# A graph network on one core: 38 more gathers behind the first pass's last one, and 32 small copies by SyncE with addresses from registers

## The reference

```python
def _gat_conv(x, src, dst, edge_attr, ...):          # twice, in the first network
    xs = (x @ lin_w.T).reshape(N, H, C)
    alpha = a_src[src] + a_dst[dst] + a_edge          # leaky ReLU follows
    m = jax.ops.segment_max(alpha, dst, num_segments=N)
    alpha = jnp.exp(alpha - m[dst])
    denom = jax.ops.segment_sum(alpha, dst, num_segments=N)
    msg = xs[src] * (alpha / (denom[dst] + 1e-16))[..., None]
    out = jax.ops.segment_sum(msg, dst, num_segments=N)
...
em = jnp.concatenate([x[src], x[dst]], axis=-1)       # once, in the second network
em = jax.nn.relu(layer_norm(em @ msg_w + msg_b, msg_g, msg_beta)) * edge_weights[:, None]
msgs = jax.ops.segment_sum(em, dst, num_segments=num_nodes)
```

## Time and profile before

| | |
|---|---|
| median of 3 runs | 8210.34 us |
| lowest and highest run | 8195.68 and 8234.33 us |
| span of the profiled execution | 6732.1 us |
| the profiled execution's own time | only its span is given |
| median less span | 1478.2 us |
| first pass, first to last of its gathers | 94.3 to 2141.3 us |
| instructions | 124645 |

### The profile page before, as it was taken

The page is one execution under the profiler, slowest core; times in us unless marked ns, Lnnn a source line. Parts: engine busy times, 40 slices in busy tenths (PEclk is TensorE's granted clock), DMA queues, the critical chain, the costliest instruction groups (busy, mean ns, idle before and its releaser), DMA issues. The chain is left out here.

```text
span 6732.1 us, 124645 instructions
## 1 busy us (share of the span) xinstructions
PE 5109.7 (76%) x33726; PEld 4567.4 (68%) x33726; DVE 4555.6 (68%) x15714; ACT 2981.2 (44%) x10333; POOL 4624.6 (69%) x4875
## 2 busy tenths in 40 slices
PE   5788887888887378888888888866676677776775
PEld 4666676676766268777777777856666666666664
DVE  5777777777777746666666665676666666666667
ACT  3444444444444322222222222255666666666666
POOL 4777777777775077777777777706777777777771
PEclk7788888888888656666666676679999999999997
DMA  8544444444443322222222222222222222222221
GB/s 173 151 116 115 115 112 114 115 115 115 114 114 85 103 61 63 64 62 63 63 63 62 64 62 63 62 86 60 54 54 53 54 54 54 54 54 54 54 54 29
DMA packets 334708, 534.90 MB, mean 79 GB/s; under 512 B 105502, under 2 KB 222767, under 8 KB 333665
## 3 DMA queue, kind: packets, MB, share of 16 engines
q0 software_dynamic: 181264, 439.20, 25.7%
q1 hardware_dynamic: 143462, 83.65, 4.6%
q10 hardware_dynamic: 9323, 4.08, 0.3%
HBM read 489.59 MB, written 42.61 MB: 79 GB/s over the span
## 5 line engine op out<-in xcount | busy, mean ns | idle before, releaser
L932 POOL DMA_INDIRECT arena<-rows,slot_src x3222 | 3079.0, 956 | 1027.3 <-issue 930.8
L722 POOL DMA_INDIRECT arena<-msg_rows,slot_src x1611 | 1521.4, 944 | 523.7 <-issue 483.9
L1130 ACT ACTIVATE arena<-psum 128x512 f32<-128x512 bf16 x808 | 480.2, 594 | 1552.3 <-PE psum L978 1528.4
L2034 PE MATMUL psum<-arena 128*128 x3232 | 704.9, 302 | 500.4 <-DMA arena<-msg_rows,slot_src 447.3
L1019 PE MATMUL psum<-arena 128*128 128x145 f32 x3232 | 978.6, 394 | 0.0
L1268 DVE TENSOR_TENSOR arena<-arena,psum 128x290 f32 x1616 | 731.2, 452 | 292.8 <-DVE arena L1268 176.6
L2034 PEld LDWEIGHTS psum<-arena 128*128 128x128 f32 x3232 | 524.6, 204 | 567.6 <-issue 567.4
L1021 PE MATMUL psum<-arena 128*128 128x145 f32 x3232 | 870.1, 360 | 0.0
L2041 ACT ACTIVATE arena<-psum 128x128 bf16<-128x128 f32 x1616 | 424.1, 277 | 754.5 <-PE psum L2036 754.4
L1205 DVE TENSOR_TENSOR arena<-arena,psum 128x512 f32<-128x512 f32 x808 | 553.6, 685 | 262.5 <-PE psum L1021 255.9
L1034 PE MATMUL psum<-arena 128*128 x3232 | 595.9, 326 | 155.9 <-ACT arena L1130 67.3
(11 more groups left out here) (360 smaller groups left out, 9590.5 us busy)
## 6 DMA issues: line engine op xcount, KB each, us to landing
arena<-rows,slot_src POOLq DMA_INDIRECT x3222
arena<-msg_rows,slot_src POOLq DMA_INDIRECT x1611
arena<-slot_keys SPq DMA_DIRECT2D x100, 128.0 KB
edge_alpha<-arena SPq DMA_DIRECT2D x50, 128.0 KB
arena<-edge_alpha SPq DMA_DIRECT2D x50, 128.0 KB
slot_keys<-lane_keys SPq DMA_DIRECT2D x24, 256.0 KB
arena<-rows SPq DMA_DIRECT2D x6, 1024.0 KB, 10.0
rows<-arena SPq DMA_DIRECT2D x4, 822.0 KB
```

The lines of the kernel that those rows point to most:

```text
L722: pool.indirect_dma_start(out=self.buffer[:, v % U, j, :], out_offset=None, in_=self.source, in_offset=bass.IndirectOffsetOnAxis(ap=K.SRC[ ...
L932: pool.indirect_dma_start(out=E.rowbuf[:, r, j, :], out_offset=None, in_=E.source, in_offset=bass.IndirectOffsetOnAxis(ap=K.SRC[:, at:at + ...
L1130: act.activation(E.onehotT[:, v % 2, :, :], E.psT, ACT.Copy).then_inc(E.turned, 1)
L2034: pe.matmul(psH[b][:, j, :], onehotT[:, b, j, :], K.by_dst[:, bass.ds(blocks(v, j), 1), :].rearrange("p b w -> p (b w)"), start=True, stop ...
```

## The change

Two functions are added, and two places call them. `spare_copies` runs in SP's queue at window 40 of the first pass, behind the wait on `topped` and ahead of the window's loads: four times it reads eight block numbers into SP's registers and issues eight copies of a_node's block of that number (128 partitions x 16 values) into `lane_keys`; then it waits for all 32. `spare_gathers` runs in POOL's queue behind the first pass's gathers: it waits for the copies, gathers 22 times from h0 into `lane_keys` (twice each: 128 rows of 128 values, and 128, 127, 126, 124, 120, 112, 96, 64, 32 and 16 rows of 64 values), waits for them, gathers 8 times 128 rows with a wait after each, then 8 times with two waits on reached semaphores and a step of a semaphore of its own ahead of each, and waits for the last. Nothing reads `lane_keys` afterwards. The semaphore is K.arrived[21]; two new ones are spare_copies and spare_steps. The SBUF table keeps its place and size.

```diff
+        self.spare = Relay(self.arrived[21], 16)
...
-        self.dstf = K.sb("lane_keys", [P, SC, P])[:, :, :]
+        lanes = K.sb("lane_keys", [P, SC, P])
+        self.dstf, K.dstf_lanes = lanes[:, :, :], lanes[:, :, :].rearrange("p c e -> p (c e)")
...
+            if E.first and z == 40:
+                spare_copies(E)
...
+def spare_copies(E):
+    sp, K = E.K.sp, E.K
+    E.keys_rest.after(sp)
+    copied = K.dmas("spare_copies")
+    lanes = K.dstf_lanes[:, 0:32 * 2 * H].rearrange("p (k w) -> p k w", k=32)
+    for n in range(4):
+        blocks = numbers_loaded(K, ET.SP, K.slot_blocks, n * LOADED, NB - 1)
+        for k in range(LOADED):
+            copied.done(sp.dma_start(lanes[:, n * LOADED + k, :].rearrange("p (b w) -> p b w", b=1),
+                                     K.a_node[:, bass.ds(blocks[k], 1), :]))
+    copied.after(sp)
+    K.spare_copied = copied
+
+def spare_gathers(E):
+    pool, K = E.K.pool, E.K
+    spare = K.spare
+    lanes = K.dstf_lanes
+    K.spare_copied.after(pool)
+    wide, half = K.h0, K.h0.rearrange("n (k w) -> (n k) w", k=2)
+    at = 0
+    for rows_, source, w in ((P, wide, F), (P, half, F // 2), (127, half, F // 2), (126, half, F // 2), (124, half, F // 2),
+                             (120, half, F // 2), (112, half, F // 2), (96, half, F // 2), (64, half, F // 2), (32, half, F // 2),
+                             (16, half, F // 2)):
+        for _ in range(2):
+            spare.done(pool.indirect_dma_start(out=lanes[0:rows_, at:at + w], out_offset=None, in_=source,
+                                               in_offset=bass.IndirectOffsetOnAxis(ap=K.SRC[0:rows_, 0:1], axis=0)))
+            at += w
+    spare.after(pool)
+    again, stepped = lanes[:, 0:F], K.sem("spare_steps")
+    for n in range(8):
+        pool.wait_ge(K.arrived[0], 16)
+        spare.done(pool.indirect_dma_start(out=again, out_offset=None, in_=wide,
+                                           in_offset=bass.IndirectOffsetOnAxis(ap=K.SRC[:, 0:1], axis=0)))
+        spare.after(pool)
+    again = lanes[:, 0:8 * F].rearrange("p (k w) -> p k w", w=F)
+    for n in range(8):
+        pool.wait_ge(K.arrived[0], 16)
+        pool.wait_ge(K.arrived[1], 16)
+        pool.sem_inc(stepped, 1)
+        spare.done(pool.indirect_dma_start(out=again[:, n, :], out_offset=None, in_=wide,
+                                           in_offset=bass.IndirectOffsetOnAxis(ap=K.SRC[:, 0:1], axis=0)))
+    spare.after(pool)
...
     edge_side_loads(E)
+    if E.first:
+        spare_gathers(E)
     edge_pe(E)
```

## The result

On the same chip and in turns with the kernel before, the changed kernel took 8240.17 us (median of 18 runs, 8203.48 to 8255.31) against 8218.29 us (18 runs, 8195.07 to 8243.9). The ratio is 1.0023, with a 95% interval of 1.0012 to 1.0033. That is within 0.5%, as forecast, and inside the range; but the interval leaves 1 out, so some 19 us (0.0023 x 8218; 10 to 27 us by the interval) have to be explained where I had summed 2.

The account below looks back on a forecast made before the run. The first pass was taken to run at POOL's pace, 5.1 us a visit, until its last gather, then PE, DVE and ACT finish. 8210.3 + 0.2 (clearing) + 2 (longer program) = 8212 us, range 8185 to 8255 us.

Parts of the forecast that it names:

- 1478 us more than the span, and the trace shows nothing of that part: Whole run: the median of 8210.34 us was taken to hold 1478 us outside the profiled span of 6732.1 us.
- Rival 4: Outside the span: loading a longer program costs 4 us, 8216 us; chance 0.78 together with the main case.
- the 2 us for a longer program: Outside the span: some 300 more instructions at 12 ns would add 4 us, of which half was taken.
- The gathers' length: POOL behind the first pass's last gather: 69.1 us of work plus a 9.1 us drain, 78.2 us in all.
- The cover: End of first pass: 89.5 us of PE, DVE and ACT work hide POOL's gathers, leaving 11 us.
- POOL's gathers don't lengthen it.: Drain of the first pass: DVE's L1268 takes 456 ns with POOL busy or idle, so its pace doesn't suffer.
- the cost is 0: Gathers behind the last gather: POOL is ready at 2219.5 us, 11 us before DVE's last add, costing 0.
- the 17 us: Added gathers: by the skill's rule each of 38 could wait 0.46 us for DVE, 6 us past the cover, +0.1%.
- The copies: SP ahead of window 40's loads: register loads, 32 copies and landing take 28.5 us, hidden, cost 0.
- The bound of 54.7 us: SP at window 40: free time for the copies before DVE's first reader waits, exceeded from 1.33 us a copy.
- Packets: Copies' 4096 packets beside the first pass's gathers: 0 us taken, 9 us as the upper bound.
- The clearing: Between the barriers: POOL clears two more semaphores at 0.08 us each, 0.2 us on the path.

Follow-up runs that it names:

- E6: The whole change with 24 instead of 8 gathers each waited for, against the kernel before, on the second, slower chip: 8351.62 us, ratio 1.0028.
- E7: Only the copies on SP, 96 instead of 32, no gathers, against the kernel before, on the second, slower chip: 8343.74 us, ratio 1.0019.
- E5: The whole change a third time, against the kernel before, on the second, slower chip: 8348.92 us, ratio 1.0033.
- E2: The 38 gathers alone, without the 32 copies and the wait for them, against the kernel before: 6741.72 us, ratio 1.0005.
- E11: The 38 gathers alone once more, without the copies, against the kernel before: 6752.73 us, ratio 1.0007.
- E4: The whole change again, against the kernel before, on a faster chip: 6747.80 us, ratio 1.0011.
- E8: The change without the copies, its first 22 gathers with other row counts, 113 to 128, on the second, slower chip: 8343.83 us, one run.

## Why the prediction held, and where its steps were off

**What bounds the kernel.** POOL's pace of 5.1 us a visit holds on the chip that the profile came from and not on the chip of the timed runs, where a visit takes 6.5 us. The step that failed is "1478 us more than the span, and the trace shows nothing of that part". The other reading, that profile and times came from chips of different pace, had no place among my rivals. Rival 4 and the 2 us for a longer program go with it: the program grew by 127 instructions, not 300, and time and span stay 2 us apart.

**The gathers' length.** Right in sum, off in its parts, which cancel. The 22 took 31.8 us (27.5 summed): the upper end of 1.35 us for a gather of fewer rows was too low, and the trace of before, with gathers of 128 rows only, could not have told. Each waited one took 2.78 us instead of 3.3, the drain 4.39 us instead of 9.1 (5.70 in E6), and the 2.7 us behind the last gather of the pass were missing. From the end of the last pass's gather to POOL ready: 2805.5 - 2730.9 = 74.6 us against 78.2.

**The cover.** I had 11 us in hand; measured are 17.9 and 23 us on chips of that pace and 30 and 32.7 us on the slower ones. Part of it is not cover but the loss itself: the drain that hides POOL is 2.5 to 17 us longer with the gathers. From the pass's last gather to DVE's drain E7 has 90.9 us and E5 108.0, so against an undisturbed drain E5 would have had 15.6 us in hand. E6 shows the other side of it: beyond the cover the cost is one to one.

**"POOL's gathers don't lengthen it."** This is the step that was wrong in kind. I had only looked at an addition in DVE, 456 ns with and without gathers, and concluded for the engines as a whole. The drain lasts some 2.5 us longer in E2 and E11 and 6.9 us in E4, 0.04 to 0.1%, and 6.5 to 17.1 us longer on the chip of E5 to E8. So "the cost is 0" was off: the answer "same" held because this loss is below 0.5%, not because there is none. The reverse, gathers held up by DVE (the 17 us worked out beside the Trainium skill, SBUF — State Buffer, on the "DVE blocks DMA" trap), isn't seen: in the changed kernel's profile those of 128 rows stay at 0.94 to 0.96 us with DVE half busy.

**The copies.** Right in sum, 29.9 us in E4 against 28.5, with parts that cancel. A copy takes 0.67 us of SP on average ((26.50 - 5.0) / 32, the three register loads between them taken off) rather than 0.51. For a register load I had taken the gap of 1.40 us from the earlier trace rows; it takes 1.65 to 1.85 us in SP's queue in E4. The last landing took 1.4 us where I had allowed 6.6. The bound of 54.7 us is bracketed, not measured: 32 copies fit in E4 and 96 do not, on a chip with more room (E7). Packets: nothing, in two comparisons. The clearing: the next phase starts 6.6 to 6.9 us behind the start of DVE's drain with and without the change (E6 apart, where POOL comes last), so 0.2 us can't be seen.

**The 19 and 27 us on the slower chips.** On chips of 6740 us the change costs 0.05 to 0.1%, and the longer drain accounts for it in size. On the slower ones it measured 1.0023 and 1.0033, 19 and 27 us. Of the 27 us (13 to 41 by the interval) the drain holds 17.1, E5 against E7; of the 19 us (10 to 27) it holds some 14, if the drain without the gathers lasts 92.7 us on that chip as well, which no run there shows. E6 has 16.4 us of longer drain and 13.4 us at the barrier, 29.8 us, where the ratio of 1.0028 gives 23 (11 to 37). E7's 1.0019 comes from another place, windows 38 to 41. So the ratio doesn't follow the amount of work, but the traces show where most of it goes.

**What stays open.** Why the drain grows, and why by 2.5 us on one chip and by 17 on another, is not known. The comparison on the slower chip rests on one trace without the gathers and three with them. Outside the drain traces of one chip differ by more than that (window 48's last product stands at 2782.9 and 2783.6 us in E5 and E6 and at 2793.6 and 2793.7 us in E7 and E8, without a reason in the edits for E8), so only the drain, cut out by its own instructions, can be compared. No unchanged copy was run against itself on such a chip.

## What to carry to other kernels

Work put behind the last job of an engine in a phase is free up to the time that the slowest engine still needs, and costs one to one beyond it; read that cover from the last instructions of both engines, and expect the others to lose time even inside it, here 2 to 7 us on the faster chips and 6 to 17 on the slower one. Before a span is set against a median, check that both come from a chip of the same pace: here time is span plus 1.7 to 2.5 us in every run, and a larger gap meant another chip. Give gathers a row count that 16 divides, or pad them to one: 127 rows cost POOL 2.7 times what 128 cost.

## What the runs showed of the hardware that was not expected

The same unchanged kernel takes 6740 us on two chips, 8218 us where the result was measured and 8326 us on the chip of E5 to E8. The slower runs have a mean granted clock of TensorE of 0.72 to 0.74 against 0.81 to 0.82, and waits in POOL whose releaser the trace doesn't show, 603.0 us at L934 in the changed kernel's profile. Why they are slower is not shown.

Gathers that nothing waits for lengthen the other engines' last 92 us of a pass to 95 to 99 us on the faster chips and to 99 to 110 us on the slower ones, while DVE's and ACT's busy time stays the same within about 1 us. POOL's time for an indirect gather goes with the divisors of its row count: 2.57 us for 127 rows, 0.95 for 128, 0.84 for 16. And reading eight values into DVE's registers takes 1.83 us, but 2.2 to 2.9 us the first time behind or beside the gathers of 127 rows, in all seven traces that have them.
